# Householder steps of an eigensolver written out on VectorE, beside a graph network's matmuls

## The reference

```
h = max(layernorm(x), 0)
Wt = adj * adj
x = x + Wt @ (relu(Wt @ (relu(Wt @ (h @ W1)) @ W2)) @ W3)        # 256 -> 512 -> 1024 -> 256
h = max(layernorm(x), 0)
_, U = eigh(D^-1/2 (D - adj) D^-1/2)                             # D from row and column sums of adj
x = x + U @ (relu((U.T @ h) @ V1 + b1) @ V2 + b2)                # 256 -> 128 -> 256
```

## Time and profile before

| | us |
|---|---|
| median of 3 runs | 2553.86 |
| the profiled execution, its time | 2556.27 |
| its span | 2554.5 |
| TensorE matmul busy in it | 2444.6 |
| VectorE busy in it | 2049.6 |

### The profile page before, as it was taken

How to read it: one execution, slowest core, us unless ns; L and a number is a source line. 1 busy time by engine, 2 the same in 40 slices (tenths; PEclk the granted TensorE clock), 3 DMA queues, 4 the chain that set the end, 5 groups by cost and what they waited for, 6 DMA issues and landing times.

```text
span 2554.5 us, 47241 instructions
## 1 busy us (share of the span) xinstructions
PE 2444.6 (96%) x11578; PEld 1984.9 (78%) x11578; DVE 2049.6 (80%) x10295; ACT 877.7 (34%) x2386; POOL 366.2 (14%) x1196
## 2 busy tenths in 40 slices
PE   6999999999999999999999999999999999999999
PEld 5777777777678777777777777888887888889998
DVE  6888888888888987777777778869999994237776
ACT  3333333333333333333333333222222222225554
POOL 1111110111111111111111112000111001013332
PEclk9999999999999999999999999999999999999999
DMA  2000000000000000000000000000000001004443
GB/s 93 26 25 25 26 10 16 25 26 26 25 20 14 26 26 17 25 25 25 25 25 9 26 26 17 25 25 25 25 25 25 25 25 58 17 1 128 131 131 111
DMA packets 90042, 90.02 MB, mean 35 GB/s; under 512 B 5376, under 2 KB 89088, under 8 KB 89856
## 3 DMA queue, kind: packets, MB, share of 16 engines
q1 hardware_dynamic: 89856, 88.23, 10.8%
HBM read 54.66 MB, written 33.55 MB: 35 GB/s over the span
## 4 chain that ended last, share of the span: by engine, by line
PE 41%; DVE 29%; issue 21%; ACT 5%; DVEq 2%; POOL 1%; SPq 0%; DMA 0%; POOLq 0%; ACTq 0%
PE ps L1134 29%; PE ps L1311 9%; DVE A L712 3%; DVE A L707 3%; DVE xrow_sb L661 3%; DVE w L700 2%; ACT root_s L450 2%; DVE sc L698 2%; DVE sc L681 2%; ACT squares L448 2%; DVE col L702 2%; DVE sc L675 2%; DVE qn L690 1%; DVE prods L692 1%; DVE sc L685 1%
## 5 line engine op out<-in xcount | busy, mean ns | idle before, releaser
L1134 PE MATMUL ps<-agg2T,w 128*128 128x256 f32 x4096 | 927.0, 379 | 0.0
L1134 PEld LDWEIGHTS ps<-agg2T,w 128*128 128x128 f32 x4096 | 761.1, 191 | 96.9
L1134 PE MATMUL ps<-w,hid2T 128*128 128x256 f32 x2048 | 464.8, 379 | 0.0
L1134 PEld LDWEIGHTS ps<-w,hid2T 128*128 128x128 f32 x2048 | 381.4, 191 | 48.8
L448 ACT ACTIVATE squares<-xrow_sb 128x121 f32<-128x121 f32 (+6 forms) x254 | 84.5, 333 | 887.9 <-DVE xrow_sb L661 887.9
L1134 PE MATMUL ps<-w,aggT 128*128 128x512 f32 x512 | 239.0, 605 | 5.4 <-ACT aggT L487 5.3
L1134 PE MATMUL ps<-weightT,hid 128*128 128x256 f32 x1024 | 234.1, 380 | 3.0 <-ACT hid L487 3.0
L350 POOL COPY Eb<-sc 128x1 f32 (+1 forms) x254 | 46.6, 183 | 1268.0 <-DVE v L679 1268.0
L487 ACT ACTIVATE hid2T<-ps 128x512 f32<-128x512 f32 x256 | 149.9, 587 | 224.2 <-PE ps L1134 224.2
L1134 PEld LDWEIGHTS ps<-weightT,hid 128*128 128x128 f32 x1024 | 190.2, 191 | 37.8 <-issue 8.9
L790 DVE RECIPROCAL pinv<-ahead 128x40 f32<-128x40 f32 (+1 forms) x768 | 215.5, 322 | 0.1
(11 more groups left out here) (306 smaller groups left out, 3620.4 us busy)
## 6 DMA issues: line engine op xcount, KB each, us to landing
xl<-in_x_dram SPq DMA_DIRECT2D x64, 256.0 KB, 2.8
xr<-in_x_dram SPq DMA_DIRECT2D x64, 256.0 KB, 2.9
x_dram<-xr SPq DMA_DIRECT2D x64, 256.0 KB, 2.3
xin<-x_dram SPq DMA_DIRECT2D x64, 256.0 KB, 2.7
out_dram<-xin SPq DMA_DIRECT2D x64, 256.0 KB, 2.3
w<-in_L_gnn_W_dram SPq DMA_DIRECT2D x1, 2048.0 KB, 9.7
w<-in_L_gnn_W_dram SPq DMA_DIRECT2D x1, 1024.0 KB, 11.5
w<-in_L_gnn_W_dram SPq DMA_DIRECT2D x1, 512.0 KB, 4.3
```

What stands on the lines that cost most here:

```text
L1134: ins = pe.matmul(dst, a, b, start=start, stop=stop)
```

## The change

On VectorE the Householder steps are no longer loops: each of the 254 steps is written out, so every wait has a constant value and every slice a constant place. The order within a step changes: `v` comes after `h`, the second copy of alpha + beta goes, the scalar `turn_w` is replaced by -1/h made before the q row, and the next column's first operation comes ahead of the sum over the row. The passes over A and the sum take the exact width k+1 to 255; the copy of the row and ACT's square keep the group's width. The updates of A signal block by block. GROUPS has ten ranges in place of seven, with 11 to 14 steps a pair in place of 10 to 14. TensorE, ACT and GpSimd keep their loops.

At pair boundaries the evacuation of both "res" units waits only for the previous pair's adds, and TensorE's first unit of a pair waits for all but the last evacuation of the pair before, its second for the last. The semaphore `evac` starts one higher, so that the other waits on it name values one higher and mean the same. A constant in the eigenvalue bounds goes from 5e-4 to 6e-4.

```diff
-HOUSE = 20
+HOUSE = 21
...
-        GROUPS = [(0, 3, 10, 0.64), (3, 7, 11, 0.64), (7, 10, 12, 0.64), (10, 11, 12, 0.64), (11, 12, 13, 0.64),
-                  (12, 19, 13, 0.62), (19, 21, 14, 0.62)]
+        GROUPS = [(0, 2, 11, 0.62), (2, 4, 11, 0.62), (4, 6, 12, 0.62), (6, 8, 12, 0.62), (8, 10, 12, 0.62),
+                  (10, 11, 12, 0.62), (11, 14, 12, 0.62), (14, 17, 12, 0.62), (17, 19, 13, 0.62), (19, 21, 14, 0.62)]
...
-                pool.memset(primer[:, i:i + 1], 0.0).then_inc(first, 1)
+                pool.memset(primer[:, i:i + 1], 0.0).then_inc(first, 2 if first is evac else 1)
...
                 if stage == "res":
-                    act.wait_ge(x1_ready, 2 * pair + j + 1)
+                    act.wait_ge(x1_ready, 2 * pair + 1)
...
-            def householder(k, k0, bl):
-                b0, c0 = bl[0], columns(k0)
+            def householder(k, c0, bl):
+                b0, here, rest = bl[0], k + 1, slice(k + 1, N)
...
                 for b in bl:
-                    ins = dve.scalar_tensor_tensor(prods[:, b, c0:N], A[:, b, c0:N], 1.0, xr[:, c0:N],
+                    ins = dve.scalar_tensor_tensor(prods[:, b, rest], A[:, b, rest], 1.0, xr[:, rest],
                                                    ALU.mult, ALU.mult, accum_out=pc[:, b:b + 1])
...
+                at(dve.tensor_scalar(h_, head, beta, beta, ALU.add, ALU.mult))
+                dve.scalar_tensor_tensor(v[:, b0:NB], ident[:, b0:NB, here], beta, xc[:, b0:NB],
                                          ALU.mult, ALU.add).then_inc(v_ready, 1)
-                at(dve.tensor_scalar(h_, alpha, beta, beta, ALU.add, ALU.mult))
-                at(dve.tensor_scalar(head, alpha, beta, None, ALU.add))
-                at(dve.tensor_scalar(alpha, alpha, beta, None, ALU.add))
                 done(8)
+                at(dve.tensor_scalar(head, head, beta, None, ALU.add))
                 at(dve.reciprocal(inv_h, h_))
-                done(11)
+                done(10)
...
+                at(dve.tensor_scalar(minus_inv_h, inv_h, -1.0, None, ALU.mult))
+                done(11)
                 dve.wait_ge(qrow, k + 1)
-                at(dve.scalar_tensor_tensor(prods[:, NB - 1, c0:N], p_q[:, c0:N], 1.0, xr[:, c0:N],
+                at(dve.scalar_tensor_tensor(col[:, b0:NB], vn[:, b0:NB], p_q[:, here:here + 1], A[:, b0:NB, here],
+                                            ALU.mult, ALU.add))
+                done(13)
+                at(dve.scalar_tensor_tensor(prods[:, NB - 1, rest], p_q[:, rest], minus_inv_h, xr[:, rest],
                                             ALU.mult, ALU.mult, accum_out=uq))
...
-                at(dve.tensor_scalar(turn_w, uq, inv_h, inv_h, ALU.mult, ALU.mult))
+                done(15)
+                at(dve.scalar_tensor_tensor(w[:, b0:NB], vn[:, b0:NB], uq, qn[:, b0:NB], ALU.mult, ALU.add))
                 done(16)
-                at(dve.scalar_tensor_tensor(w[:, b0:NB], v[:, b0:NB], turn_w, qn[:, b0:NB], ALU.mult, ALU.add))
+                at(dve.scalar_tensor_tensor(col[:, b0:NB], w[:, b0:NB], head, col[:, b0:NB], ALU.mult, ALU.add))
                 done(17)
...
                 for b in bl:
-                    ins = dve.scalar_tensor_tensor(A[:, b, c0:N], p_q[:, c0:N], vn[:, b:b + 1], A[:, b, c0:N],
-                                                   ALU.mult, ALU.add)
-                at(ins)
+                    at(first_update(b), b0 + 1)
                 done(19)
                 for b in bl:
-                    ins = dve.scalar_tensor_tensor(A[:, b, c0:N], xr[:, c0:N], w[:, b:b + 1], A[:, b, c0:N],
-                                                   ALU.mult, ALU.add)
-                at(ins)
+                    at(second_update(b), b0 + 1)
...
-            for (first, last, steps, share), k0 in zip(GROUPS, FIRST_STEP):
-                with dve.Fori(first, last) as t:
-                    for s in range(steps):
-                        householder(steps * t + (k0 - steps * first) + s, k0, blocks(k0))
-            for k in TAIL:
-                householder(k, k, range(NB - 1, NB))
+            for (first, last, steps, _), k0 in zip(GROUPS, FIRST_STEP):
+                for k in range(k0, k0 + steps * (last - first)):
+                    householder(k, columns(k0), blocks(k0))
...
-                    pe.wait_ge(evac, NU * pair + 1)
+                    pe.wait_ge(evac, NU * pair + j + 1)
...
-                    pe.wait_ge(evac, NU * pair + max(need, i - 4) + 2)
+                    pe.wait_ge(evac, NU * pair + max(need, i - 4) + 3)
```

More of the change, by code:

```diff
@@ L375, in add_x @@
                 pool.wait_ge(load_xr[j], 16 * pair + 16)
-                pool.wait_ge(evac, NU * pair + AT["res", j, 0] + 2)
+                pool.wait_ge(evac, NU * pair + AT["res", j, 0] + 3)
                 pool.tensor_tensor(xres[:, j, :, :], xres[:, j, :, :], res[:, j, :, :], ALU.add).then_inc(x1_ready, 1)
@@ L641, in _, with at, first_update, second_update @@
                                               ALU.mult, ALU.add))
-            def householder(k, k0, bl):
-                b0, c0 = bl[0], columns(k0)
+            def householder(k, c0, bl):
+                b0, here, rest = bl[0], k + 1, slice(k + 1, N)
                 def done(i):
                     dve.wait_ge(house_v, HOUSE * k + i + 1)
-                def at(ins):
-                    ins.then_inc(house_v, 1)
-                half, inv_len, h_, beta, inv_h, head, scaled, uq, turn_w = (sc[:, i:i + 1] for i in range(1, 10))
+                def at(ins, n=1):
+                    ins.then_inc(house_v, n)
+                half, inv_len, h_, beta, inv_h, minus_inv_h, scaled, uq = (sc[:, i:i + 1] for i in range(1, 9))
                 square, length = root_s[:, 0:1], root_s[:, 1:2]
-                here = bass.ds(k + 1, 1)
-                alpha = xr[:, here]
+                head = xr[:, here:here + 1]
+                def first_update(b):
+                    return dve.scalar_tensor_tensor(A[:, b, rest], p_q[:, rest], vn[:, b:b + 1], A[:, b, rest],
+                                                    ALU.mult, ALU.add)
+                def second_update(b):
+                    return dve.scalar_tensor_tensor(A[:, b, rest], xr[:, rest], w[:, b:b + 1], A[:, b, rest],
+                                                    ALU.mult, ALU.add)
                 done(0)
@@ L663, in householder @@
                 for b in bl:
-                    ins = dve.scalar_tensor_tensor(prods[:, b, c0:N], A[:, b, c0:N], 1.0, xr[:, c0:N],
+                    ins = dve.scalar_tensor_tensor(prods[:, b, rest], A[:, b, rest], 1.0, xr[:, rest],
                                                    ALU.mult, ALU.mult, accum_out=pc[:, b:b + 1])
                 at(ins)
-                at(dve.tensor_scalar(half, alpha, 0.0, 0.5, ALU.is_ge, ALU.subtract))
+                at(dve.tensor_scalar(half, head, 0.0, 0.5, ALU.is_ge, ALU.subtract))
                 dve.wait_ge(root, k + 1)
@@ L676, in householder @@
                 done(7)
[L677 removed]
+                dve.scalar_tensor_tensor(qcol[:, b0:NB], A[:, b0:NB, here], beta, pc[:, b0:NB],
                                          ALU.mult, ALU.add).then_inc(q_ready, 1)
[L679 removed]
+                at(dve.tensor_scalar(h_, head, beta, beta, ALU.add, ALU.mult))
+                dve.scalar_tensor_tensor(v[:, b0:NB], ident[:, b0:NB, here], beta, xc[:, b0:NB],
                                          ALU.mult, ALU.add).then_inc(v_ready, 1)
[L681 to L683 removed]
                 done(8)
+                at(dve.tensor_scalar(head, head, beta, None, ALU.add))
                 at(dve.reciprocal(inv_h, h_))
[L686 removed]
+                done(10)
                 dve.wait_ge(v_ready, k + 1)
@@ L693, in householder @@
+                done(13)
+                at(dve.scalar_tensor_tensor(prods[:, NB - 1, rest], p_q[:, rest], minus_inv_h, xr[:, rest],
                                             ALU.mult, ALU.mult, accum_out=uq))
-                done(13)
-                at(dve.scalar_tensor_tensor(col[:, b0:NB], vn[:, b0:NB], p_q[:, here],
-                                            A[:, b0:NB, here].squeeze(2), ALU.mult, ALU.add))
-                done(14)
-                at(dve.tensor_scalar(turn_w, uq, inv_h, inv_h, ALU.mult, ALU.mult))
+                done(15)
@@ L699, in householder @@
+                at(dve.scalar_tensor_tensor(w[:, b0:NB], vn[:, b0:NB], uq, qn[:, b0:NB], ALU.mult, ALU.add))
                 done(16)
-                at(dve.scalar_tensor_tensor(w[:, b0:NB], v[:, b0:NB], turn_w, qn[:, b0:NB], ALU.mult, ALU.add))
+                at(dve.scalar_tensor_tensor(col[:, b0:NB], w[:, b0:NB], head, col[:, b0:NB], ALU.mult, ALU.add))
                 done(17)
-                at(dve.scalar_tensor_tensor(col[:, b0:NB], w[:, b0:NB], head, col[:, b0:NB], ALU.mult, ALU.add))
@@ L703, in householder @@
-                done(18)
-                dve.tensor_tensor(xc[:, b0:NB], col[:, b0:NB], below[:, b0:NB, here].squeeze(2),
```

(7 more changed lines are left out.)

4 lines of the change are left out of this document (1 added, 3 removed).

## The result

The changed kernel takes 2439.22 us (median of 4 runs, 2438.79 to 2440.41), the kernel before on the same chip 2554.44. The ratio is 0.9551 with a 95% interval of 0.9534 to 0.9567: 4.5% faster, 115 us. The forecast was 2465, and its range ended at 2442, so the gain came out 26 us larger than forecast and 3 us beyond the range.

What follows compares the result with a forecast made beforehand. VectorE and TensorE hand work to each other, VectorE late in the Householder stage. New stage: 1398 + 10 + 12 + 24 = 1444 against 1524, 80 us; with 9 behind it 89; 2554.5 - 89 - 0.6 = 2465 us, range 2442 to 2510.

Steps and rivals of the forecast that it cites:

- The likeliest case: Whole kernel: Householder stage shortens to TensorE's floor plus start, uneven steps and pair ends; 2465 us (2448 to 2485), chance 0.64.
- C: Rival for the Householder stage: TensorE fed perfectly, floor plus start only, 1408 us; kernel 2429 us, chance 0.08.
- B: Rival: VectorE stays the bound in the Householder stage's first half, the jumps alone come through; 2505 us, chance 0.18.
- D: Rival: TensorE is the bound already, leaving only the pair boundaries to gain; 2535 to 2550 us, chance 0.04.
- E: Rival: fetching the written-out Householder steps starves VectorE, making the kernel slower; 2620 us, chance 0.04.
- stage of before, read to 1542: Householder stage of the unchanged kernel, from step 0's row copy at 17.90 to the last step at 1542: 1524.1 us.
- TensorE's floor: Householder stage: 21 pairs at 62.39 us plus 128 steps at 0.44 and 126 at 0.25, 1398.0 us.
- uneven work between steps: Householder stage, first 70 steps: 0.15 us charged on each and little after, 12 us.
- pair ends: Householder stage: GpSimd's adds still hold VectorE, 2.0 us for six pairs, 0.8 for the other 15; 24 us.
- start: Start of the Householder stage: VectorE's first reciprocal waits for ACT's root behind layer 0's first norm, 10 us.
- boundary waits behind the stage: Ten pair boundaries after step 253: TensorE waits for the last but one evacuation, saving 0.9 us each, 9 us.
- Steps reordered: VectorE's Householder step: next column before the sum shortens 1.36 us to 1.09, 0.27 saved; one scalar less, 0.10.

Runs made afterwards that it cites:

- Experiment 5: The changed kernel with the old order behind the q row (sum over the row first, then col, `turn_w`, w): 2442.81 us, ratio 0.9556.
- experiment 9: The changed kernel with two dependent 128-column VectorE operations, results unread, added in each of the 126 one-block steps: 2443.4 us, ratio 0.9565.
- experiment 10: The changed kernel with GpSimd's add of x cut to 4 of 256 columns, so the sum is incomplete: 2414.16 us, ratio 0.9451.
- experiment 1: The kernel before with only VectorE's Householder steps written out, in old order, widths, groups and boundary waits: 2467.94 us, ratio 0.9652.
- experiment 4: The kernel before with the steps written out and the new boundary waits; order, widths and groups old: 2450.5 us, ratio 0.9588.
- experiment 8: The changed kernel with the old seven groups (10 steps a pair first, 14 last): 2443.83 us, ratio 0.9554.
- experiment 3: The kernel before with GpSimd's add of x cut to 4 of 256 columns, the rest left out: 2511.19 us, ratio 0.9822.

## Why the prediction was right in kind and too small

The likeliest case was the right mechanism, and the truth lies between it (2448 to 2485) and its neighbour C, TensorE fed perfectly (2429). B needed VectorE to bound the first half; in after the plain steps there take 6.05, 5.71 and 5.62 us, within 0.1 of TensorE's share. (Experiment 5 is a weak test of B, since it lengthens the step by some 0.1 us only; experiment 9 tests the second half.) D, TensorE the bound already, and E, starved by the fetching of written-out code, are refuted by the 4.5%. Most marks named beforehand appeared: no "issue" before the copy, xc 1.11 us behind col, the step windows up to step 199, one held operation per add, no idle time at the pair starts behind the stage. The stage length did not: 1427 us for 1444.

The forecast span was 2554.5 - 89 = 2465.5, the measured one 2437.7. The 27.8 between them, by the prediction's own steps:

| step of the prediction | forecast | measured | us |
|---|---|---|---|
| stage of before, read to 1542 | 1524.1 | 1531.0 | 6.9 |
| TensorE's floor (0.44 and 0.25 a step) | 1398.0 | 1388.4 | 9.6 |
| uneven work between steps | 12 | 7.2 | 4.8 |
| pair ends | 24 | 21.6 | 2.4 |
| start | 10 | 10 | 0 |
| boundary waits behind the stage | 9 | 13.4 | 4.4 |

The floor of 1388.4 is 21 pairs of 62.39 with 128 two-block steps at 0.414 and 126 one-block steps at 0.20, by experiment 10's pairs. The 7.2 are what is then left: 1427.2 - 1388.4 - 10 - 21.6; experiment 10's first six pairs, steps 0 to 67, hold 6.2 of them. The sum of the last column is 28.1; 0.3 is rounding at the stage's start.

**The step that failed most plainly** is the price of a step on TensorE: "I take 0.25 a step (half would be 0.22; the weight load may not halve)". The choice went the wrong way and nothing checked it, 126 times over; it measured 0.20, below either value. Together with 0.414 for 0.44 the floor came out 9.6 us too high, the largest term of the table. With both prices right and the stage closed where it ends, the forecast would have been near 2449. **The boundaries** were priced by one row of 1.01 us, though the earlier trace rows shows a 1.73 too; the ten idle times behind the stage that ACT's last evacuation ended ran from 0.63 to 2.15 us, one of them followed by a half-clock spell, and sum to 11.9.

**The parts, taken singly, were priced worse than the whole.** The prediction gave 39 us to the jumps and let constants, reordering, exact widths and even groups shorten the rest. The written-out code alone brought 87. Of the 0.27 us a step that "Steps reordered" saves, after shows 0.25, but experiments 1 and 5 give only 0.14 of it to the order, so that the 1.11 us behind col came near the forecast partly by luck. The forecast came near all the same because it was built from the far side: TensorE's floor plus what breaks in. With TensorE at its floor in most of the stage, a VectorE step that is 0.1 us shorter or longer matters in a few pairs only, and so each of the three, undone, costs 0 to 5 us. Together they are worth about 11.

**The clock was overlooked.** "GpSimd's second add then meets xc, ... TensorE idles 2.15 us for it" stopped one step short: 3.4 us at half clock follow. This changed nothing in the sum, since before's stage was taken whole and the new stage was built at full clock. But it is part of why removing either the jumps or the adds paid more than their idle time: some 10 us by the pairs with and without a spell. The times agree with this without being exact. Over 22 runs of the kernel before, in which the mean granted clock lies between 0.992 and 0.996, the span falls by 1.4 us for each 0.001 of clock (correlation -0.67; by chip 0.6, 1.6 and 1.6), where 2554/1000 = 2.6 would be all of it. The clock is given to three digits only, which flattens that slope.

**Open.** How experiment 1's 87 us divide is read from steps of its trace, not isolated: no run had constants with the jumps kept, and that the 31.5 us of the jumps count in full is assumed. Why a jump leaves VectorE idle for 2.25 us no run shows either; the broken prefetch that the prediction names was not tested. Why nine of the fifteen idle times of 1.95 us or more in before's stage led to a half-clock spell and six did not isn't settled; one of 2.11 us in experiment 4 did not, one of 2.11 us in experiment 8 did. The 11 us of order, widths and groups were not divided further.

## What to carry to other kernels

Build the forecast from the floor of the engine that will bound the kernel after the change, price that floor from pairs of windows that differ in one thing only, and close each window where the work ends. Look for a loop's backward jump in the waits as "issue" ahead of the first operation of its body, and write the loop out on the engine whose jump falls on the critical path; the others can keep theirs. Where two short stalls fall together in one place, look at the clock column behind them: removing either may return more than its own idle time. And before reading a result off a reversed edit, measure in its trace that the step changed by what was meant.

## What the runs showed of the hardware that was not expected

- Of fifteen idle times of TensorE of 1.95 to 2.33 us in before's stage, nine were followed by 3.4 us at half the granted clock. In the stages of experiment 3 and of after, with idle times of at most 1.7 us, it never happened.
- Waits and slices given by registers cost VectorE 0.3 us a step over constant ones, at three spots of some 25 operations: 0.35 against 0.26 us from beta to qcol, 0.34 against 0.25 to xc, and about 0.1 to the next row copy. Other operations that waited for a register value (w: 0.30 us behind its scalar in both kernels) cost nothing more.
- At a loop's backward jump VectorE stood idle for 2.25 us on average, at its exit for none. TensorE, ACT and GpSimd still jump in after; TensorE's idle time at the pair ends there (0.64 us) is ended by xc, and with the adds cut short (experiment 10) it has none there, where 0.3 was charged.
- In a kernel in which TensorE is busy for 98%, GpSimd's 1.26 us adds still cost 1.0 us a pair on average; experiment 10's 25 us are the largest single gain that a run showed beyond the change.
